# A causal mask by a product in PSUM, in place of GpSimd's selection behind the exponentials

## The chip, the core and the metric

The kernel runs on one core of a Trainium2 chip. A core has a matrix engine (TensorE, PE in the profile, with PEld for its weight loads), VectorE (DVE), ScalarE (ACT), GpSimd (POOL) and SyncE (SP, which issues the DMAs here). Products accumulate in PSUM; all else lives in SBUF. The metric is the device time of one execution in microseconds.

## The reference

Two pre-norm layers over x of shape (2, 1024, 512), in float32:

- x += attention(layernorm(x)): 32 query heads and 8 key/value heads of 16 channels, rotary embedding, causal softmax over 1024 positions, output projection
- x += layernorm(x) @ kernel + bias
- x += a decay-weighted linear attention (32 heads of 128 channels) with norm and gate
- x += a linear layer with a routed low-rank addition

The change is in the first of them. What it must compute there:

```
scores = einsum('bqhd,bkhd->bhqk', xq, xk) / sqrt(16)
scores = where(causal, scores, -inf)
probs  = softmax(scores)
out    = einsum('bhqk,bkhd->bqhd', probs, xv)
```

## The kernel before

The program is a series of stages written out by hand, each with its own instruction stream for every engine and with semaphores between them. `softmax_attend` (lines 596 to 896) is the second. It works through 16 groups, one for each batch and key/value head, with 4 query heads each (REP). Positions are cut into 8 tiles of 128.

Each group is done twice over. First the scores with queries on the partitions (`scores_for_max`, lines 818 to 831), only to get each row's maximum: PE writes up to 1024 columns, DVE reduces them (line 789). The diagonal tile gets its causal mask there by a second product into the same PSUM columns, identity times `mask_s` (line 829); `mask_s` holds 0 where the key is not later than the query and -1e30 elsewhere, in bf16. The maxima are cut into three bf16 parts, turned, and sent by a DMA into three further rows of the queries (`QT`, 96 + 3 rows), so that the next product already subtracts them.

Then the scores transposed, with keys on the partitions (`scores`, lines 833 to 847). `UNITS` lists nine units of a group, each 512 columns wide: a unit is one or two pieces (key tile, first query tile, number of query tiles). Eight pieces begin on the diagonal (key equals q). A unit is computed once for each head j: PE writes one of two PSUM buffers `ps_t` (line 844), ACT takes the exponential into a ring of five units `E` (line 752) and signals `e_ready`. The score product waits until the exponential two before it is over. When the four heads of a unit are there, GpSimd sets the first 128 columns of each diagonal piece to 0 above the diagonal, all four heads at once (line 733), and signals `causal`. `times_v` (lines 849 to 869) multiplies with V and a column of ones (line 862), as four float32 products of 32 output columns per piece; before it PE waits for `e_ready` (line 852), for `causal` (line 853) and, at the first key tile, for the output buffer (line 858). The finished outputs are copied by ACT (line 759), turned back by PE (line 893) and divided by DVE.

The order on PE, ACT and DVE is one list, `ORDER`: events sorted by a position worked out from the columns that the maxima read, with a product with V placed 1.625 units behind the end of its unit's scores. GpSimd's stream is not in the list; it follows the units. In this stage it has eight subtractions of weights ahead of its selections, and nothing behind them.

Of the kernel before, what the change touches and what calls it, by code (L numbers as in the profile page):

```python
# [23 lines left out]
ALU = mybir.AluOpType  # L24
# [3 lines left out]
P = 128  # L28
# [5 lines left out]
REP = HEADS // KV_HEADS  # L34
# [155 lines left out]
KEPT = 3  # L190
# [405 lines left out]
def softmax_attend(nc, pairs, stored, prefetch, E, V, O, QT, KT, Q_dram, K_dram, load_group, q_in, k_in, ident_f, ident_b,  # L596
# [4 lines left out]
    with ExitStack() as ctx:  # L601
        core = Core(nc, ctx)
# [5 lines left out]
        UNITS = [  # L608
            [(0, 0, 4)], [(1, 1, 3), (3, 3, 1)], [(0, 4, 4)], [(2, 2, 2), (6, 6, 2)],
            [(1, 4, 4)], [(2, 4, 4)], [(3, 4, 4)], [(4, 4, 4)], [(5, 5, 3), (7, 7, 1)],  # L610
        ]
        HALF_DONE = (3, 8)
        NU = len(UNITS)
        ALL = GROUPS * NU
# [7 lines left out]
        RING = E.shape[1]  # L622
# [27 lines left out]
        for G in range(GROUPS):  # L650
            summed = [NU * G + HALF_DONE[half] + 1 + VALUES_LAG for half in range(2)]
            placed += [(summed[half] + 1.1, 3, ("keep", G, half)) for half in range(2)]
            placed.append((summed[1] + 1.6, 4, ("back", G)))
        ORDER = [event for _, _, event in sorted(placed, key=lambda one: one[0:2])]
        IN_S = {e: n for n, e in enumerate(e for e in ORDER if e[0] in ("max", "turn_max", "back"))}

# [7 lines left out]
        ps_t = [pairs[2][:, 0, :], pairs[2][:, 1, :]]  # L664
# [13 lines left out]
        e_ready = core.sem("att_e_ready")  # L678
        pv_done = core.sem("att_pv_done")
        kept = core.sem("att_kept")  # L680
        den_ready = core.sem("att_den_ready")
        causal = core.sem("att_causal")

        def diagonals(units):

            return sum(key == q for U in range(units) for key, q, _ in UNITS[U % NU])

        def max_rows(slot):
            return slot[0:MT, 0, 0:P // 2].bitcast(BF16)
# [6 lines left out]
        with nc.Block() as block:  # L696
# [22 lines left out]
            @block.gpsimd  # L719
            def _(pool):  # L720
                for n, (_, w_hi, w_lo) in enumerate(prefetch):
                    for c in range(KC):
                        pool.wait_ge(w_split, KC * n + c + 1)
                        nc.gpsimd.tensor_tensor(w_lo[:, c, :], w_raw[n][:, c, :], w_hi[:, c, :], ALU.subtract
                                                ).then_inc(w_rest, 1)
                zero = pool.to_reg(0.0)
                for U in range(ALL):
                    pool.wait_ge(e_ready, REP * U + REP)
                    a = 0
                    for key, q, count in UNITS[U % NU]:  # L730
                        if key == q:
                            e = E[:, U % RING, :, a:a + P]
                            nc.gpsimd.affine_select(e, e, [[0, REP], [1, P]], ALU.is_ge, zero, base=0,  # L733
                                                    channel_multiplier=-1).then_inc(causal, 1)
                        a += count * P

            @block.scalar
            def _(act):
# [77 lines left out]
            @block.tensor  # L816
            def _(pe):
                def scores_for_max(slot, g, k):

                    q, heads, step = SLOTS[k]  # L820
                    flat = slot.rearrange("p b n -> p (b n)")
                    for h, j in enumerate(heads):
                        for a in range(0, (q + 1) * P, 512):
                            b = min(a + 512, (q + 1) * P)
                            to, diagonal = h * step, b == (q + 1) * P
                            mm = pe.matmul(flat[:, to + a:to + b], QT[0:STACK, g % KEPT, j, q * P:(q + 1) * P],  # L826
                                           KT[0:STACK, g % KEPT, a:b], start=True, stop=not diagonal)
                            if diagonal:
                                mm = pe.matmul(flat[:, to + b - P:to + b], ident_b[:, :], mask_s[:, :],  # L829
                                               start=False, stop=True)  # L830
                    mm.then_inc(s_ready, 1)

                def scores(U, j):

                    g, u = divmod(U, NU)
                    i = REP * U + j
                    if u == 0 and j == 0:
                        pe.wait_ge(max_in[g % KEPT], 16 * (g // KEPT + 1))
                    if i >= 2:
                        pe.wait_ge(e_ready, i - 1)  # L840
                    a = 0
                    for key, q, count in UNITS[u]:
                        b = a + count * P
                        mm = pe.matmul(ps_t[i % 2][:, a:b], KT[:, g % KEPT, key * P:(key + 1) * P],  # L844
                                       QT[:, g % KEPT, j, q * P:(q + count) * P], start=True, stop=True)
                        a = b
                    mm.then_inc(t_ready, 1)

                def times_v(U):

                    g, u = divmod(U, NU)
                    pe.wait_ge(e_ready, REP * U + REP)
                    pe.wait_ge(causal, diagonals(U + 1))
                    a = 0
                    for key, q, count in UNITS[u]:
                        half = q // HALF
                        if key == 0 and g >= 1:
                            pe.wait_ge(kept, 2 * (g - 1) + half + 1)
                        b, c = a + count * P, (q % HALF) * P
                        first = (SEQ_TILES * g + key) * V_COLS  # L860
                        for j in range(REP):
                            mm = pe.matmul(ps_oT[half][WIDE * j:WIDE * (j + 1), c:c + b - a], V[:, first:first + WIDE],
                                           E[:, U % RING, j, a:b], start=(key == 0), stop=(u == HALF_DONE[half]),
                                           skip_group_check=True)
                        a = b
                    mm.then_inc(pv_done, 1)

                for event in ORDER:
                    if event in IN_S:
                        n = IN_S[event]  # L870
                        slot = ps_s[n % 2]
                        if n >= 2:
                            pe.wait_ge(s_read, n - 1)
                    if event[0] == "max":
                        _, g, k = event
                        if k == 0:
                            pe.wait_ge(k_in[g % KEPT], 48 * (g // KEPT + 1))
                            pe.wait_ge(q_in[g % KEPT], 48 * (g // KEPT + 1))
                        scores_for_max(slot, g, k)
                    if event[0] == "turn_max":  # L880
                        g = event[1]
                        pe.wait_ge(max_step, STEPS * (g + 1))
                        pe.transpose(max_rows(slot), mx_part[:, g % 2, :, :, :].rearrange("p m h q -> p (m h q)"),
                                     ident_b[:, :]).then_inc(s_ready, 1)
                    if event[0] == "score":
                        scores(*event[1:])
                    if event[0] == "values":
                        times_v(event[1])
                    if event[0] == "back":
                        g = event[1]  # L890
                        pe.wait_ge(kept, 2 * g + 2)
                        for q in range(SEQ_TILES):
                            mm = pe.transpose(slot[:, q // HALF, (q % HALF) * P:(q % HALF + 1) * P],
                                              oT[:, g % 2, q // HALF, (q % HALF) * P:(q % HALF + 1) * P],
                                              ident_f[:, :])
                        mm.then_inc(s_ready, 1)
# [1471 lines left out]
```

## Time and profile before

| | |
|---|---|
| Median of three runs | 3093.97 us (3090.79 to 3095.16) |
| The profiled execution | 3091.87 us, its span 3090.1 us |
| Mean granted TensorE clock | 0.980 |
| Busy in the span | PE 2953.2 us, PEld 2350.5, DVE 1598.5, ACT 1440.7, POOL 1413.1 |
| The stage's score products, line 844 | 768, first at 154.7, last at 643.0 us |
| Exponentials, line 752 | 576, 596 ns each |
| Selections, line 733 | 128, first at 159.8, last at 644.5 us, 634 ns each |

Times of rows are counted from the start of the span. A row of the timeline may merge several instructions of one form; its second number is the time from the first's start to the last's end. Starts of successive products are sounder than their ends, which are modelled. What stands in square brackets is how long the engine was idle before, and what released it; "issue" means nothing that the profile shows. PE and its weight loads are listed apart.

### The profile page before, as it was taken

The page shows a single profiled execution, that of the slowest core. Times are in us where ns is not written, and L with a number is a line of the kernel's source. Part 1 is how long each engine was busy: PE and PEld are TensorE (multiplying, and loading weights), DVE is VectorE, ACT ScalarE, POOL GpSimd, SP SyncE. Part 2 cuts the span into 40 slices and gives each one's busy share as a digit, 9 for nine tenths or more (in the row PEclk, how much of TensorE's full clock was granted, in tenths as well). Part 3 has the DMA queues.
Part 4 walks back from the last instruction along what each step waited for, and adds up shares of the span by engine and source line. Part 5 has one row for each costly group of instructions (what it writes and reads, how often), then busy time and mean ns, then how long its engine had stood idle before and what let it go on. Part 6 is the DMA issues. An engine that isn't in the chain of part 4 may idle for free. (4 is left out here: it accounts for less than half of the span.)

```text
span 3090.1 us, 54423 instructions
## 1 busy us (share of the span) xinstructions
PE 2953.2 (96%) x18200; PEld 2350.5 (76%) x18200; DVE 1598.5 (52%) x2742; ACT 1440.7 (47%) x2510; POOL 1413.1 (46%) x1243
## 2 busy tenths in 40 slices
PE   7799999989999999999999989999999999999958
PEld 6444444358888888888888878888888888888846
DVE  6677777637444444334444446434444443444478
ACT  5266666644444444444444444444444444444421
POOL 5411111122555555555555554554555555455531
PEclk9799999999999999999999998999999999999979
DMA  4411212002111111111111120111111111111121
GB/s 142 120 27 28 40 27 40 15 32 72 45 37 44 44 37 44 48 44 37 44 44 37 44 95 28 46 53 38 39 49 37 37 48 51 37 42 47 52 87 55
DMA packets 102712, 149.58 MB, mean 48 GB/s; under 512 B 24228, under 2 KB 44452, under 8 KB 102376
## 3 DMA queue, kind: packets, MB, share of 16 engines
q1 hardware_dynamic: 102632, 148.52, 16.5%
q8 instruction: 49, 0.80, 0.1%
q14 instruction: 31, 0.25, 0.0%
HBM read 129.74 MB, written 18.35 MB: 48 GB/s over the span
## 5 line engine op out<-in xcount | busy, mean ns | idle before, releaser
L1860 PE MATMUL bank<-l_xC,l_w_T 128*128 128x512 f32 x2304 | 561.9, 393 | 0.0
L1860 PEld LDWEIGHTS bank<-l_xC,l_w_T 128*128 128x128 f32 x2304 | 428.1, 188 | 87.9
L1860 PE MATMUL bank<-l_xT,l_w_T 128*128 128x512 f32 x1728 | 453.2, 401 | 6.5 <-DVE l_gT L1753 6.5
L789 DVE TENSOR_REDUCE att_max<-bank 128x1 f32<-128x640 f32 (+6 forms) x352 | 354.7, 1027 | 107.0 <-PE bank L829 103.4
L752 ACT ACTIVATE att_exp<-bank 128x512 f32<-128x512 f32 x576 | 323.6, 596 | 148.8 <-PE bank L844 142.7
L1753 DVE TENSOR_TENSOR l_kT<-bank,l_qT 128x512 f32<-128x512 f32 x128 | 88.5, 692 | 577.8 <-PE bank L1860 577.8
L1829 PEld LDWEIGHTS bank<-l_v_T,l_xT 128*128 128x128 f32 x3072 | 376.5, 191 | 7.4 <-issue 5.0
L1829 PE MATMUL bank<-l_v_T,l_xT 128*128 128x256 f32 x3072 | 377.8, 285 | 4.4 <-PEq L1013 2.7
L1860 PEld LDWEIGHTS bank<-l_xT,l_w_T 128*128 128x128 f32 x1728 | 310.6, 188 | 69.6 <-DVE l_gT L1753 12.7
L1875 PE MATMUL bank<-l_o_T,l_y_hi 128*128 128x512 f32 x1024 | 324.1, 393 | 0.0
L1595 POOL TENSOR_TENSOR l_qd<-l_qT,l_q_decay 128x1024 f32<-128x1024 f32 x64 | 151.9, 2373 | 372.7 <-ACT l_qT L1658 372.7
L733 POOL TENSOR_SCALAR_AFFINE_SELECT att_exp<-att_exp 128x512 f32<-128x512 f32 x128 | 78.9, 634 | 424.1 <-ACT att_exp L752 424.1
L1605 POOL TENSOR_TENSOR l_sq_sum<-l_sq_sum,l_sq 128x512 f32<-128x512 f32 x128 | 164.9, 1288 | 189.9 <-ACT l_sq L1671 189.9
L1564 POOL TENSOR_TENSOR l_w_T<-l_sums,l_w_T 128x1024 fp32r<-128x1024 f32 x96 | 230.9, 2405 | 38.1 <-ACT l_w_T L1631 37.9
L1800 DVE TENSOR_TENSOR l_acc<-l_acc,bank 128x512 f32<-128x512 f32 x256 | 169.8, 686 | 107.0 <-PE bank L1875 102.1
L844 PE MATMUL bank<-att_QT,att_KT 99*128 99x512 bf16 (+3 forms) x768 | 211.9, 332 | 12.1 <-ACT att_exp L752 5.7
L1875 PEld LDWEIGHTS bank<-l_o_T,l_y_hi 128*128 128x128 f32 x1024 | 192.4, 188 | 39.4
L826 PE MATMUL bank<-att_KT,att_QT 96*128 96x512 bf16 (+3 forms) x768 | 205.4, 345 | 17.0 <-PEq L84 13.0
L1641 ACT ACTIVATE l_v<-bank 128x256 f32<-128x256 f32 x256 | 98.3, 384 | 243.1 <-PE bank L1829 243.1
L1875 PE MATMUL bank<-l_o_T,l_y_lo 128*128 128x512 f32 x512 | 199.5, 390 | 0.0
L1829 PE MATMUL bank<-l_sc,l_v 128*128 128x128 f32 x1024 | 190.5, 278 | 9.1 <-POOL l_qd L1595 9.1
L1564 POOL TENSOR_TENSOR l_w_T<-l_w_raw,l_w_T 128x512 fp32r<-128x512 f32 x192 | 191.2, 1010 | 0.0
(281 smaller groups left out, 5067.1 us busy)
## 6 DMA issues: line engine op xcount, KB each, us to landing
l_w_raw<-in_L_attn_qkv_w SPq DMA_DIRECT2D x196, 256.0 KB, 2.8
l_w_raw<-in_L_attn_gate_w SPq DMA_DIRECT2D x66, 256.0 KB, 2.7
l_o_raw<-in_L_attn_out_w SPq DMA_DIRECT2D x33, 512.0 KB, 3.5
query_parts<-att_exp SPq DMA_DIRECT2D x48, 128.0 KB
att_QT<-query_parts SPq DMA_DIRECT2D x16, 384.0 KB, 5.5
X<-x_rows SPq DMA_DIRECT2D x3, 2048.0 KB, 13.6
X<-in_L_attn_x SPq DMA_DIRECT2D x4, 1024.0 KB, 11.2
att_QT<-query_parts SPq DMA_DIRECT2D x16, 256.0 KB, 5.5
```

The lines of the kernel that those rows point to most:

```text
L752: nc.scalar.activation(E[:, U % RING, j, :], ps_t[i % 2], ACT.Exp, scale=SCALE).then_inc(e_ready, 1)
L789: dve.tensor_reduce(mx[:, g % 2, heads[0]:heads[-1] + 1, q], columns(slot, q, len(heads), step), AX_X, ALU.max).then_inc(s_read, 1)
L826: mm = pe.matmul(flat[:, to + a:to + b], QT[0:STACK, g % KEPT, j, q * P:(q + 1) * P], KT[0:STACK, g % KEPT, a:b], start=True, stop=not dia ...
L844: mm = pe.matmul(ps_t[i % 2][:, a:b], KT[:, g % KEPT, key * P:(key + 1) * P], QT[:, g % KEPT, j, q * P:(q + count) * P], start=True, stop= ...
L1564: nc.gpsimd.tensor_tensor(low, src, split_of(event, 0)[1], ALU.subtract).then_inc(sems.split_lo, 1)
L1595: nc.gpsimd.tensor_tensor(qd[:, :].rearrange("p (c n) -> p c n", n=P), qT[:, h, :].rearrange("p (c n) -> p c n", n=P), buf.q_decay[:, h, : ...
L1605: nc.gpsimd.tensor_tensor(sq_sum[:, half(event[2])], sq_sum[:, half(event[2])], sq[:, :], ALU.add).then_inc(sems.sq_added, 1)
L1641: nc.scalar.activation(v[:, event[1], :], ps_p[p_bank(event)][:, 0:HP * P], ACT.Silu).then_inc(sems.p_read[p_bank(event)], 1)
L1800: dve.tensor_tensor(acc[:, t, :], acc[:, t, :], ps_p[t % NP_][:, :], ALU.add).then_inc(sems.p_read[t % NP_], 1)
L1829: mm = pe.matmul(out, lhs, rhs, start=(n == 0), stop=(n == len(pairs) - 1))
L1860: mm = pe.matmul(ps_p[p_bank(event)][:, :], w[:, SLOT[pair], LEFT[i], P * c:P * c + P], quarter(i, x, xc, c), start=(n == 0 and i in (1, 6 ...
L1875: mm = pe.matmul(ps_p[t % NP_][:, :], y[:, h, chunk(t)], w[:, h, :], start=(h == 0 and n == 0), stop=(h == 1 and n == 2))
```

## The change

The selection, its semaphore and the wait for it go. Each score product whose piece begins on the diagonal now leaves its accumulation open, and a second product adds the mask to its first 128 columns: `mask_s` as the stationary operand and the bf16 identity as the moving one, which gives the mask transposed, with keys on the partitions. The exponential of -1e30 times the scale is 0. The list `ORDER` and all other operands are the same.

```diff
--- before.py
+++ after.py
@@ -679,11 +679,6 @@
         pv_done = core.sem("att_pv_done")
         kept = core.sem("att_kept")
         den_ready = core.sem("att_den_ready")
-        causal = core.sem("att_causal")
-
-        def diagonals(units):
-
-            return sum(key == q for U in range(units) for key, q, _ in UNITS[U % NU])
 
         def max_rows(slot):
             return slot[0:MT, 0, 0:P // 2].bitcast(BF16)
@@ -723,16 +718,6 @@
                         pool.wait_ge(w_split, KC * n + c + 1)
                         nc.gpsimd.tensor_tensor(w_lo[:, c, :], w_raw[n][:, c, :], w_hi[:, c, :], ALU.subtract
                                                 ).then_inc(w_rest, 1)
-                zero = pool.to_reg(0.0)
-                for U in range(ALL):
-                    pool.wait_ge(e_ready, REP * U + REP)
-                    a = 0
-                    for key, q, count in UNITS[U % NU]:
-                        if key == q:
-                            e = E[:, U % RING, :, a:a + P]
-                            nc.gpsimd.affine_select(e, e, [[0, REP], [1, P]], ALU.is_ge, zero, base=0,
-                                                    channel_multiplier=-1).then_inc(causal, 1)
-                        a += count * P
 
             @block.scalar
             def _(act):
@@ -842,7 +827,9 @@
                     for key, q, count in UNITS[u]:
                         b = a + count * P
                         mm = pe.matmul(ps_t[i % 2][:, a:b], KT[:, g % KEPT, key * P:(key + 1) * P],
-                                       QT[:, g % KEPT, j, q * P:(q + count) * P], start=True, stop=True)
+                                       QT[:, g % KEPT, j, q * P:(q + count) * P], start=True, stop=key != q)
+                        if key == q:
+                            mm = pe.matmul(ps_t[i % 2][:, a:a + P], mask_s[:, :], ident_b[:, :], start=False, stop=True)
                         a = b
                     mm.then_inc(t_ready, 1)
 
@@ -850,7 +837,6 @@
 
                     g, u = divmod(U, NU)
                     pe.wait_ge(e_ready, REP * U + REP)
-                    pe.wait_ge(causal, diagonals(U + 1))
                     a = 0
                     for key, q, count in UNITS[u]:
                         half = q // HALF
```

Line numbers behind the stage's declarations move: the scores' product is line 829 after the change (844 before), its mask line 832, the maxima's two products 811 and 814 (826 and 829), and the product with V 848 (862).

PE, within the interval between two products with V that holds two units with diagonals. `att_QT` and `att_KT` are the queries and keys, `bank` is PSUM, `mask_query_key` is `mask_s`. Before:

```order
L862 MATMUL bank<-att_exp,V_columns 32x512 x3
L844 MATMUL bank<-att_QT,att_KT 128x384 [waits att_e_ready]
L844 MATMUL bank<-att_QT,att_KT 128x128
L826 MATMUL bank<-att_KT,att_QT 128x512 [waits att_s_read]
L826 MATMUL bank<-att_KT,att_QT 128x128
L829 MATMUL bank<-mask_query_key,identity_bf 128x128
L844 MATMUL bank<-att_QT,att_KT 128x512 [waits att_e_ready,att_max_in0]
L844 MATMUL bank<-att_QT,att_KT 128x512 [waits att_e_ready]
L826 MATMUL bank<-att_KT,att_QT 128x512 [waits att_s_read]
```

and with the change:

```order
L848 MATMUL bank<-att_exp,V_columns 32x512 x3
L829 MATMUL bank<-att_QT,att_KT 128x384 [waits att_e_ready]
L832 MATMUL bank<-identity_bf,mask_query_key 128x128
L829 MATMUL bank<-att_QT,att_KT 128x128
L832 MATMUL bank<-identity_bf,mask_query_key 128x128
L811 MATMUL bank<-att_KT,att_QT 128x512 [waits att_s_read]
L811 MATMUL bank<-att_KT,att_QT 128x128
L814 MATMUL bank<-mask_query_key,identity_bf 128x128
L829 MATMUL bank<-att_QT,att_KT 128x512 [waits att_e_ready,att_max_in0]
L832 MATMUL bank<-identity_bf,mask_query_key 128x128
L829 MATMUL bank<-att_QT,att_KT 128x512 [waits att_e_ready]
L832 MATMUL bank<-identity_bf,mask_query_key 128x128
```

Each score piece that begins on the diagonal is followed by a product of 128 columns, here four within three scores; nothing has changed places.

PE, one interval of the last group, where no maxima stand between the scores. `att_exp` is `E`, `V_columns` is V with its ones. Before:

```order
L862 MATMUL bank<-att_exp,V_columns 32x384 [waits att_causal,att_e_ready]
L862 MATMUL bank<-att_exp,V_columns 32x384 x3
L862 MATMUL bank<-att_exp,V_columns 32x128 x4
L844 MATMUL bank<-att_QT,att_KT 128x256 [waits att_e_ready]
L844 MATMUL bank<-att_QT,att_KT 128x256
L844 MATMUL bank<-att_QT,att_KT 128x512 [waits att_e_ready] x3
L862 MATMUL bank<-att_exp,V_columns 32x512 [waits att_kept,att_causal,att_e_ready]
```

and with the change:

```order
L848 MATMUL bank<-att_exp,V_columns 32x384 [waits att_e_ready]
L848 MATMUL bank<-att_exp,V_columns 32x384 x3
L848 MATMUL bank<-att_exp,V_columns 32x128 x4
L829 MATMUL bank<-att_QT,att_KT 128x256 [waits att_e_ready]
L832 MATMUL bank<-identity_bf,mask_query_key 128x128
L829 MATMUL bank<-att_QT,att_KT 128x256
L832 MATMUL bank<-identity_bf,mask_query_key 128x128
L829 MATMUL bank<-att_QT,att_KT 128x512 [waits att_e_ready] x3
L848 MATMUL bank<-att_exp,V_columns 32x512 [waits att_kept,att_e_ready]
```

The first score of this interval has two diagonal pieces and gets two masks; the product with V waits for one semaphore less.

## Rows read from the trace of the kernel before

**Rows 1.** Busy us (instructions), 350 to 450 us: PE, PEld, DVE, ACT, POOL, clock, DMA.

```profile
350.00:450.00 100.00, 97.56 (x757) 42.71 (x756) 77.19 (x94) 68.35 (x123) 16.02 (x26) 1.00 0.16 31
```

**Rows 2.** The page's costliest groups: GpSimd's selection.

```profile
L733 POOL TENSOR_SCALAR_AFFINE_SELECT att_exp<-att_exp 128x512 f32<-128x512 f32 x128 | 78.9, 634 | 424.1 <-ACT att_exp L752 424.1
```

**Rows 3.** Timeline, end of attention: start us, us, instruction xcount [idle before <-releaser].

```profile
643.17 1.07 PE L862 MATMUL bank<-att_exp,V_columns 128*32 128x512 f32 x8
643.28 0.60 ACT L752 ACTIVATE att_exp<-bank 128x512 f32<-128x512 f32 x1 [0.72 <-PE bank L844]
...
645.31 1.07 PE L862 MATMUL bank<-att_exp,V_columns 128*32 128x384 f32 x16 [1.07 <-POOL att_exp L733]
```

**Rows 4.** Waits, 200 to 600 us: us in total, times, longest.

```profile
ACT att_exp L752 <- PE bank L844: 119.2, 143, 1.2
PEld bank L844 <- ACT att_exp L752: 87.1, 182, 0.8
...
PEld bank L862 <- issue: 28.3, 130, 0.3
```

**Rows 5.** Timeline of PE, two products with V one group apart.

```profile
414.45 1.07 PE L862 MATMUL bank<-att_exp,V_columns 128*32 128x384 f32 x16
...
445.26 1.07 PE L862 MATMUL bank<-att_exp,V_columns 128*32 128x384 f32 x16
```

**Rows 6.** Timeline of all engines, the interval that begins at 430.94.

```profile
430.62 0.11 PEld L844 LDWEIGHTS bank<-att_QT,att_KT 99*128 99x128 bf16 x2 [0.22 <-ACT att_exp L752]
...
430.94 1.06 PE L862 MATMUL bank<-att_exp,V_columns 128*32 128x512 f32 x8
...
431.94 0.39 PE L844 MATMUL bank<-att_QT,att_KT 99*128 99x384 bf16 x2
...
432.17 0.44 PE L826 MATMUL bank<-att_KT,att_QT 96*128 96x512 bf16 x2
...
432.37 2.23 ACT L752 ACTIVATE att_exp<-bank 128x512 f32<-128x512 f32 x4 [0.72 <-PE bank L844]
...
433.02 0.10 PEld L844 LDWEIGHTS bank<-att_QT,att_KT 99*128 99x128 bf16 x1 [0.47 <-ACT att_exp L752]
```

**Rows 7.** Line 853: all, and from 423 to 424.6: min/median/max ns, first to last start.

```profile
L853 PEldq EVENT_SEMAPHORE  x114: 51/51/51, 163.9 to 645.2; - x114
...
L853 PEldq EVENT_SEMAPHORE  x1: 51/51/51, 423.9 to 423.9; - x1
```

**Rows 8.** Timeline, entry to the product with V at 424.65.

```profile
424.50 0.22 PE L829 MATMUL bank<-mask_query_key,identity_bf 128*128 128x128 bf16 x1
...
424.65 1.07 PE L862 MATMUL bank<-att_exp,V_columns 128*32 128x512 f32 x8
```

**Rows 9.** Timeline, first and last of eight 128-column products of the maxima.

```profile
453.79 0.22 PE L826 MATMUL bank<-att_KT,att_QT 96*128 96x128 bf16 x1
...
454.20 0.22 PE L829 MATMUL bank<-mask_query_key,identity_bf 128*128 128x128 bf16 x1
```

**Rows 10.** Groups of line 829 from 200 to 860 us: its weight loads.

```profile
L829 PEld LDWEIGHTS bank<-mask_query_key,identity_bf 128*128 128x128 bf16 x421 | 40.8, 97 | 29.7
```

**Rows 11.** Timeline, one row from each of four other intervals.

```profile
426.73 0.10 PEld L844 LDWEIGHTS bank<-att_QT,att_KT 99*128 99x128 bf16 x1 [0.31 <-ACT att_exp L752]
...
429.55 0.63 PE L844 MATMUL bank<-att_QT,att_KT 99*128 99x384 bf16 x4
...
436.85 0.11 PEld L844 LDWEIGHTS bank<-att_QT,att_KT 99*128 99x128 bf16 x2 [0.36 <-ACT att_exp L752]
...
443.36 1.09 PE L893 MATMUL bank<-identity_f,att_oT 128*128 128x128 f32 x8 [0.31 <-DVE att_max L789]
```

**Rows 12.** Timeline of the last group, without maxima.

```profile
615.86 1.06 PE L862 MATMUL bank<-att_exp,V_columns 128*32 128x512 f32 x8
...
617.94 0.88 PE L844 MATMUL bank<-att_QT,att_KT 99*128 99x512 bf16 x2 [0.47 <-ACT att_exp L752]
...
618.75 1.07 PE L862 MATMUL bank<-att_exp,V_columns 128*32 128x512 f32 x8
```

## The prediction

> **What bounds the kernel now.** I read a window of the attention stage first, then the page's row of the operation that goes, the waits, and last a timeline through one key/value group. Only softmax attention is touched, some 493 us of the span. A window of 100 us inside it shows PE 97.6, DVE 77.2, ACT 68.4 and POOL 16.0 us busy, at a granted clock of 1.00 [rows 1]: POOL is far from being the bound, and since the ends of products are modelled, PE's share tells only that it is rarely without work; what holds it must be read from the order of starts. POOL's 128 selections take 634 ns each, 78.9 us in all, and POOL itself idled 424 us for the exponentials before them [rows 2]. Did anybody wait for POOL? One product did, for 1.1 us, at the very end of the stage [rows 3]. The waits name another pair: the exponentials wait for the scores, 119 us between 200 and 600 us, and the weight loads of the scores wait for the exponentials, 87 us [rows 4].
>
> The timeline shows the beat. The stream is periodic: the product with V that starts at 414.45 us has its like at 445.26, so a group takes 30.81 us [rows 5], and 16 of them are 493 us. A group has nine intervals from one product with V to the next. Each interval holds four scores; I call them first (behind the product with V) to fourth (ahead of the next), with products for the maximum between them. Take the interval from 430.94 to 434.22 [rows 6]: the first score starts at 431.94, its exponential at 432.37, 0.43 later; the third score is held until that exponential is over (loads at 433.02, after 0.47 idle on ACT), since the scores have two PSUM buffers; from there PE runs without a gap through third score, maxima and fourth score to the product with V. So the path is: first score, its exponential, third score, all PE work to the next first score. PE work between the first and the third score costs nothing as long as the idle before the third lasts.
>
> **What is removed.** (a) 128 selections: hidden behind all else but the last. After them the last product with V starts at 645.31. The last exponential ends at 643.88 and PE streams the product before from 643.17 for 1.0 us, so without POOL it starts at about 644.2. That gives 1.1 us back [rows 3]. (b) The wait for POOL at each product with V. It leaves a 51 ns semaphore instruction in front of 114 of them [rows 7]. Is it paid? There is a gap: two score products of 384 and 128 columns need 0.23 us from start to the next start (431.94 to 432.17), but 0.32 when the product with V comes next (loads at 430.62, that product at 430.94), so 0.09 is lost at each entry [rows 6]. But before the product at 424.65 the semaphore instruction is done at 423.9, 0.7 us ahead, and still 424.50 to 424.65 is 0.15 for a 128-column product where 0.06 is its pace [rows 7 to 9]. The gap belongs to something else in the entry, such as the change to 32-column float32 weights, and I count nothing for the wait. If it were all due to it, 114 x 0.09 = 10.3 us would come back; that is the other end. A loss is excluded: an instruction less on the queue adds no work.
>
> **What is added.** 8 diagonal tiles x 4 heads x 16 groups = 512 bf16 products of 128 columns with their weight loads, each directly behind a score product and into the same PSUM columns. The trace has the like: in the maxima, a mask product follows a score product on the same columns with no gap. From 453.79 to 454.20 there are seven steps of such pairs, 0.41 us, so one costs 0.0586 us, weight load included, since its 97 ns run beside the product before [rows 9, 10]. A bound above is that load in full, 97 ns; below, nothing for a mask that falls into idle time.
>
> Which masks lie on the path? A diagonal tile is masked for its four heads, and these take all four places of the beat. By interval of one group (start, length; masks in it, on the path), with one row each for four of them [rows 11]:
> - 424.65, 3.06: 3, 2. The second score's falls into idle time (third loads at 426.73 after 0.31 on ACT).
> - 427.71, 3.23: 7, 7. Second and third score run back to back (429.55, x4, 0.63 us), so nothing hides them; the loads of the fourth waited 0.22 for ACT [rows 6], but PE was streaming maxima until then, and I give nothing off for it.
> - 430.94, 3.28: 5, 4. Only the second's is hidden [rows 6].
> - 434.22, 3.34: 7, 5. The fourth score waits for the second's exponential (436.85, 0.36 on ACT), so first, second and fourth count and the two masks of the third fall into idle time.
> - 437.56, 3.01: 2, 2, both on the first score, as the first of 430.94.
> - 440.57, 4.69: 6, 4. The second's two fall into the 0.31 us in which the transposes wait for DVE's maximum (443.36).
> - 445.26, 3.11: 2, 2, as at 437.56.
> - 448.37 and 451.48: none.
>
> Together 32 masks, of which 26 count: 26 x 0.0586 = 1.52 us a group, times 15 groups = 22.9 us. The 16th group has no maxima beside it and beats at 2.89 us (615.86 to 618.75), purely in the loop of PE and ACT: the third score is held for the first's exponential (0.47 us of PE idle at 617.94), the fourth for the second's, which is why the two take 0.88 us [rows 12]. There the masks of the first and of the fourth score count: 16 x 0.0586 = 0.9 us. The exponentials themselves keep their number and their width.
>
> **Sum.** 22.9 + 0.9 - 1.1 = 22.7 us. The profiled execution took 3091.87 us (span 3090.1), so 3114.6; the median of the runs shown is 3093.97, 2.1 above it, which gives 3116.7. I forecast 3116. The rivals below are put against the median. Measurement tells about 0.2%, 6.2 us, from no change; 22.7 us is 0.7%.
>
> A rule that speaks against the price: rows 9 show 0.0586 us for a 128-column product together with its load. The Trainium skill ("TensorE: Matmul & The Clock Gate", Back-to-back issue gap) states about 81 ns per product for a sustained stream of load and product pairs at 128 columns. By that figure the 406 masks on the path would be 32.9 us and the sum 31.8, an estimate; the trace disagrees, and the sum above goes by the trace.
>
> **Rivals.**
> 1. The entry gap was the semaphore's: 10.3 us come back, net +12.4, 3106.4. For it: a gap in all entries, and one such instruction per entry. Against it: the instruction at 423.9 ran 0.7 us ahead. Chance 0.12.
> 2. TensorE is the bound throughout, no idle hides anything: 512 x 0.0586 - 1.1 = +28.9, 3122.9. For it: 97.6% busy. Against it: the idle before the third score. Chance 0.08.
> 3. The mask's weight load is not hidden behind the score product, whose contraction has 99 rows and not 128: 406 x 0.097 - 1.1 = +38.3, 3132.3 (406 is 15 x 26 + 16). Against it: loads of the maxima's masks beside 96-row products cost nothing extra. Chance 0.05. The 81 ns that the Trainium skill states (same page and section) would lie between this and rival 2.
> 4. Only the latency to the first exponential counts, PE's other masks being absorbed: 128 first scores x 0.0586 - 1.1 = +6.4, 3100.4, at the edge of no change. For it: the loads of most third scores wait for ACT [rows 4]. Against it: no gap on PE between third score and product with V. Chance 0.05.
> 5. The other side, faster: the removed wait holds the loads of the V product. The trace puts 28.3 us of PEld idle between 200 and 600 us before them to no releaser, 130 times at 0.2 each [rows 4]. If the loads moved up by all of it, some 114 x 0.22 = 25 us would come back against 22.7 spent: -2; with the masks absorbed as in 4 it is 6.4 - 25 = -19, 3075. It decides once an entry gets back more than 22.7 / 114 = 0.20 us. Against it: PE is streaming the score in most of that time; only 0.09 of an entry is really empty, which is under 0.20. Chance 0.02.
>
> **Numbers.** The forecast has 0.68, with 3111 to 3120 as its own range (the place of each mask, and the 2 us between the profile and the median). The range 3104 to 3125 takes in rivals 1 and 2, and leaves out 3, 4 and 5. Faster by over 0.2%: 0.02. Within 0.2%: 0.05 (rival 4). Slower: 0.93.
>
> **What would show it.** The new product has 512 instances at a pace of 0.06 us behind each score, no selection is left on POOL, and the group period rises from 30.81 to about 32.33 us, while intervals without a diagonal (448.37, 451.48) keep 3.11 and 3.98. The entry to the product with V keeps 0.32 us without its semaphore instruction; if it falls to 0.23, rival 1 holds. In the last group, intervals with one diagonal tile take 3.01 and with two 3.12, those without stay at 2.89. The stages after attention only shift. I am wrong if the group period rises by less than 0.9 or by more than 2 us, or if the entries become shorter.

## The result, and the profile after

| | before | changed |
|---|---|---|
| median | 3092.38 us (4 runs, 3090.43 to 3095.16) | 3114.65 us (4 runs, 3114.48 to 3115.34) |
| profiled execution, its span | 3091.87, 3090.1 us | 3114.48, 3112.7 us |

The ratio is 1.0072 (95% interval 1.0054 to 1.0089): the change makes the kernel 22.3 us slower, where 22.7 were forecast.

The page of the changed kernel: engine totals, then the groups of the exponentials and of the scores (busy us, mean ns of one, idle before and its releaser).

```profile
PE 2983.1 (96%) x18712; PEld 2384.2 (77%) x18712; DVE 1602.1 (51%) x2742; ACT 1443.7 (46%) x2510; POOL 1335.2 (43%) x1115
...
L737 ACT ACTIVATE att_exp<-bank 128x512 f32<-128x512 f32 x576 | 325.8, 596 | 169.3 <-PE bank L832 104.2
...
L829 PE MATMUL bank<-att_QT,att_KT 99*128 99x512 bf16 (+3 forms) x768 | 225.2, 332 | 8.5 <-ACT att_exp L737 5.1
```

GpSimd's selections [rows 2] are gone from the page and PE's busy time has grown by 29.9 us, from 2953.2 to 2983.1. The exponentials take the 596 ns that they took. The same window of the attention stage as before (columns as in rows 1):

```profile
350.00:450.00 100.00, 98.76 (x830) 47.07 (x830) 73.76 (x91) 66.44 (x118) 0.00 (x0) 1.00 0.19 37
```

POOL stands still, where it had 16.02 us [rows 1]; PE has 830 products in place of 757, and DVE and ACT do less in the same time. ACT did not get slower, it is fed more slowly. The mask products by themselves (minimum, median and maximum ns, first and last start):

```profile
L832 PEld LDWEIGHTS bank<-identity_bf,mask_query_key x512: 96/98/151, 153.1 to 664.3; 128*128 128x128 bf16 x171
L832 PE MATMUL bank<-identity_bf,mask_query_key x512: 219/219/314, 153.6 to 664.4; 128*128 128x128 bf16 x171
```

The waits from 200 to 600 us (total, times, longest) answer to [rows 4]:

```profile
ACT att_exp L737 <- PE bank L832: 82.1, 85, 1.3
PEld bank L829 <- ACT att_exp L737: 74.7, 151, 0.8
ACT att_exp L737 <- PE bank L829: 41.5, 51, 1.1
PEld bank L848 <- issue: 18.6, 87, 0.3
```

ACT waited 119.2 us for the scores; now it is 82.1 + 41.5 = 123.6, two thirds of it for the mask product that closes a score. The same 400 us hold 12.4 groups now and held 13.0, so both are a little more per group than these sums suggest. The waits of the scores' loads for ACT fell from 87.1 to 74.7 (6.7 us a group before, 6.0 now): part of the masks went into that idle time.

**One interval, instruction by instruction.** The same interval of the same group as in [rows 6]; it begins at 442.45 now, where it began at 430.94 (PE, PEld and ACT; start, duration):

```profile
442.45 1.07 PE L848 MATMUL bank<-att_exp,V_columns 128*32 128x512 f32 x8
...
443.45 0.34 PE L829 MATMUL bank<-att_QT,att_KT 99*128 99x384 bf16 x1
...
443.63 0.22 PE L832 MATMUL bank<-identity_bf,mask_query_key 128*128 128x128 bf16 x1
...
443.69 0.22 PE L829 MATMUL bank<-att_QT,att_KT 99*128 99x128 bf16 x1
...
443.75 0.22 PE L832 MATMUL bank<-identity_bf,mask_query_key 128*128 128x128 bf16 x1
...
443.80 0.43 PE L811 MATMUL bank<-att_KT,att_QT 96*128 96x512 bf16 x2
...
444.00 2.34 ACT L737 ACTIVATE att_exp<-bank 128x512 f32<-128x512 f32 x4 [0.84 <-PE bank L832]
...
444.65 0.10 PEld L829 LDWEIGHTS bank<-att_QT,att_KT 99*128 99x128 bf16 x1 [0.41 <-ACT att_exp L737]
...
445.97 0.64 PE L848 MATMUL bank<-att_exp,V_columns 128*32 128x512 f32 x4
```

First score 443.45, mask 443.63, second piece 443.69, its mask 443.75, maxima 443.80: the same two pieces took 0.23 us to the next start and take 0.35, 0.06 for each mask, loads included. The exponential starts 0.55 behind the first score, not 0.43, and the third score's load, still held by ACT, 1.20 behind it, not 1.08. From there every mask pushes the next product. The interval is 3.52 us long, 3.28 before.

**Where the 22.6 us of the span lie.** The product of the maxima just ahead of the first score starts at 154.06 before and 152.52 after; the last transposes of the stage start at 647.17 and 667.23. So the stage takes 21.60 us more, what is ahead of it took 1.54 us less in this execution, and what is behind it 2.54 us more. The work on both sides is the same, and the granted clock is not: from 110 to 162 us it was 0.51 before and 0.54 after, and behind the stage it was lower after. Windows behind the stage, changed kernel first, then before (busy us of PE, PEld, DVE, ACT, POOL, then the granted clock):

```profile
665.00:670.00 5.00, 2.76 (x34) 1.67 (x27) 1.05 (x2) 0.80 (x2) 0.00 (x0) 0.94 0.00 0
670.00:675.00 5.00, 4.45 (x15) 3.47 (x14) 1.38 (x2) 1.17 (x2) 0.00 (x0) 0.50 0.68 192
675.00:680.00 5.00, 5.00 (x23) 4.09 (x22) 1.29 (x2) 0.59 (x1) 0.00 (x0) 0.88 0.20 75
```

```profile
645.00:650.00 5.00, 2.46 (x27) 1.71 (x28) 1.05 (x2) 0.58 (x1) 0.16 (x1) 1.00 0.00 0
650.00:655.00 5.00, 4.03 (x24) 3.25 (x22) 1.29 (x2) 1.07 (x2) 0.00 (x0) 1.00 0.63 201
655.00:660.00 5.00, 5.00 (x26) 4.14 (x25) 2.25 (x4) 1.69 (x3) 0.40 (x1) 1.00 0.16 63
```

In the pause between the stages the clock fell from its upper level (2.4 GHz, 1.00) to the lower (0.50) in this execution of the changed kernel, and in the one of the kernel before it did not. It does not follow the masks: in the run without any mask in the scores (`e2_neither`) it fell too, and in the run with all of them but none in the maxima (`e7`), as in those with masks for one head, it did not. There is one profile of each kernel, so what decides it stays open.

### The profile page after: what moved, and what is told of

It is laid out like the page before. It is cut to its first block and busy times, and to the rows that moved or that the text cites. A ratio compares the mean times of both kernels' runs of the same rounds, so it can differ in the third digit from the quotient of the medians.

```text
span 3112.7 us, 55154 instructions
## 1 busy us (share of the span) xinstructions
PE 2983.1 (96%) x18712; PEld 2384.2 (77%) x18712; DVE 1602.1 (51%) x2742; ACT 1443.7 (46%) x2510; POOL 1335.2 (43%) x1115
## 5 line engine op out<-in xcount | busy, mean ns | idle before, releaser
L829 PE MATMUL bank<-att_QT,att_KT 99*128 99x512 bf16 (+3 forms) x768 | 225.2, 332 | 8.5 <-ACT att_exp L737 5.1
```

## The experiments

Starts of the product with V were read from each trace, and from them the nine intervals of a group. Apart from the first group and the passage to the last they repeat from group to group to 0.01 us, while whole runs scatter by some us, so they carry the verdicts. Intervals bear the start they had before; all in us. "Masks" is how many of the scores' masks fall into it, "foretold" what the prediction added.

| interval | masks | before | foretold | changed | e3 twice | e4 second | e5 first | e6 | e7 |
|---|---|---|---|---|---|---|---|---|---|
| 424.65 | 3 | 3.06 | +0.12 | 3.17 | 3.29 | 3.06 | 3.06 | 2.94 | 3.06 |
| 427.71 | 7 | 3.23 | +0.41 | 3.56 | 3.95 | 3.35 | 3.28 | 3.11 | 3.40 |
| 430.94 | 5 | 3.28 | +0.23 | 3.52 | 3.74 | 3.34 | 3.40 | 3.17 | 3.40 |
| 434.22 | 7 | 3.34 | +0.29 | 3.63 | 3.90 | 3.46 | 3.40 | 3.22 | 3.52 |
| 437.56 | 2 | 3.01 | +0.12 | 3.12 | 3.24 | 3.01 | 3.12 | 2.95 | 3.07 |
| 440.57 | 6 | 4.69 | +0.23 | 4.93 | 5.16 | 4.69 | 4.69 | 4.57 | 4.82 |
| 445.26 | 2 | 3.11 | +0.12 | 3.23 | 3.34 | 3.12 | 3.23 | 3.06 | 3.18 |
| 448.37 | 0 | 3.11 | 0 | 3.11 | 3.11 | 3.10 | 3.11 | 3.05 | 3.04 |
| 451.48 | 0 | 3.98 | 0 | 3.99 | 3.98 | 3.99 | 3.99 | 3.68 | 3.69 |
| group | 32 | 30.81 | +1.52 | 32.27 | 33.71 | 31.11 | 31.28 | 29.75 | 31.17 |

**e1, masks added, selections kept.** The kernel before with the added half of the change alone (the score product's first line is left out here):

```diff
   ...
-  QT[:, g % KEPT, j, q * P:(q + count) * P], start=True, stop=True)
+  QT[:, g % KEPT, j, q * P:(q + count) * P], start=True, stop=key != q)
+  if key == q:
+      mm = pe.matmul(ps_t[i % 2][:, a:a + P], mask_s[:, :], ident_b[:, :], start=False, stop=True)
```

> The mask products are added and the selections with their wait stay. Path theory (26 of 32 masks of a group on PE's path at 0.0586 us, the wait in front of the product with V free): +23.8 us over the kernel before, about 3116, that is 1.1 us above the changed kernel, and that 1.1 us at the last product with V. Rival 1 (the entry gap belongs to the wait for GpSimd): the wait is back, so 10.3 us above the changed kernel as well, about 3126. Rival 2 (TensorE bound throughout) gives the same as the changed kernel plus 1.1.

Measured: 3116.64 us against 3092.95 (ratio 1.0078, 1.0062 to 1.0095), 2.0 above the changed kernel where 1.1 were foretold (single runs spread over 3.6 us), with the same group period to the hundredth, 32.27. The wait for GpSimd stands in front of every product with V here and costs nothing until the last (PE, last two products with V):

```profile
664.58 1.06 PE L864 MATMUL bank<-att_exp,V_columns 128*32 128x512 f32 x8
666.72 1.07 PE L864 MATMUL bank<-att_exp,V_columns 128*32 128x384 f32 x16 [1.07 <-POOL att_exp L733]
```

They are 2.14 us apart, as at the end of the kernel before [rows 3], with the 1.07 us wait for POOL. Rival 1, which put this kernel 10 us higher, is out.

**e2, neither.** The changed kernel with its mask product taken out (`stop=True`, no second product), so that only the removed half of the change is left.

> The selections and their wait go and no mask is added: the causal mask inside the diagonal tiles is left out of the exponentials. Path theory: 1.1 us less than before, about 3091.3, group period 30.81 as before, entry to the product with V still 0.32 us behind a 512 column pair. Rival 1: 11.4 us less than before, 3081, group period 30.0. Rival 5 (the loads of the product with V were held by the wait): up to 25 us less.

Measured: 3090.95 us against 3092.95 (ratio 0.9993, 0.9983 to 1.0002), group period 30.82. By the whole runs that is no difference that can be told from none, and by the period removing selections and wait is worth nothing but the end (2.73 us from the product before the last to the transposes, 4.00 before). With e1 the two halves add up: +23.7 and -2.0 are 21.7, beside 22.3 measured together. Rival 5 is out as well. This run also had the fall of the clock behind the stage:

```profile
648.00:653.00 5.00, 4.04 (x15) 3.12 (x14) 1.29 (x2) 1.07 (x2) 0.00 (x0) 0.66 0.64 186
```

**e3, each mask twice.** The changed kernel with one line more:

```diff
+  mm = pe.matmul(ps_t[i % 2][:, a:a + P], mask_s[:, :], ident_b[:, :], start=False, stop=False)
   mm = pe.matmul(ps_t[i % 2][:, a:a + P], mask_s[:, :], ident_b[:, :], start=False, stop=True)
```

> Each mask product stands twice. Path theory: the second mask again costs where the first did, 26 of 32 per group, since the idle of third scores and of the transposes is not used up (0.13 to 0.47 us left): +23.8 us over the changed kernel, 3138.4, group period 32.28 + 1.5. Rival 2 (nothing is hidden): 512 x 0.0586 = +30, 3144.7. If hidden places were used up by the first mask, it would be the same 30.

Measured: 3137.14 us (ratio 1.0142, 1.0126 to 1.0159), 22.5 above the changed kernel, where 23.8 were foretold; the group period grows by another 1.44 us, after 1.46. Intervals with two masks on the path (424.65, 437.56, 445.26) grow by 0.11 this time, so a second mask costs 0.055 us, a little less than a first. 32 of them would make 1.76; 26 make 1.43. The same masks are hidden the second time, and rival 2 is out. The interval 427.71, where every mask was held to count, grew by 0.33 at first and grows by 0.39 now, which is seven masks of 0.055: what took one in the first time is used up.

**e4 and e5, one mask in four.** The mask product for one head only: `if key == q and j == 0` makes it the second score behind a product with V, `j == 3` the first. Both have 128 mask products.

> Only the head whose score is the second behind a product with V gets its mask product (128 of 512); the other three heads are left without a mask in the exponentials. Path theory: only the intervals that begin like 427.71 and 434.22 grow, by 2 masks each, 4 x 0.0586 x 15 = 3.5, less 1.1 at the end: +2.4 us over before, about 3094.8. Rival 2: 128 x 0.0586 - 1.1 = +6.4, 3098.8.

> Only the head whose score is the first behind a product with V gets its mask product (128 of 512); the other three heads are left without a mask in the exponentials. As many products as in the run with the second score only. Path theory: all of them count, 15 x 8 x 0.0586 + 8 x 0.0586 - 1.1 = +6.4 us over before, 3098.8, 4.0 above the run with the second score only. Rival 2 (PE bound throughout): both runs the same.

Measured: second score 3095.10 us against 3092.95 (ratio 1.0006, 0.9997 to 1.0016), first score 3098.21 against 3092.42 (1.0024, 1.0014 to 1.0034). The periods say it more sharply: +0.30 and +0.47 us a group for eight masks each. The place decides, not the number. First scores: 0.47 / 8 = 0.059, all of them on the path. Second scores: nothing in the intervals 424.65 and 440.57, as foretold, two masks each in 427.71 and 434.22, as foretold, but also 0.06 in 430.94, where the prediction had it hidden. The timeline of that interval in the run with the second score masked, shortened to the rows that decide (ACT, PE and PEld):

```profile
434.11 2.29 ACT L737 ACTIVATE att_exp<-bank 128x512 f32<-128x512 f32 x4 [0.72 <-PE bank L829]
...
434.24 0.38 PE L829 MATMUL bank<-att_QT,att_KT 99*128 99x512 bf16 x1
...
434.46 0.22 PE L832 MATMUL bank<-identity_bf,mask_query_key 128*128 128x128 bf16 x1
434.75 0.10 PEld L829 LDWEIGHTS bank<-att_QT,att_KT 99*128 99x128 bf16 x1 [0.41 <-ACT att_exp L737]
...
435.26 0.22 PE L814 MATMUL bank<-mask_query_key,identity_bf 128*128 128x128 bf16 x1
...
435.37 0.39 PE L829 MATMUL bank<-att_QT,att_KT 99*128 99x512 bf16 x1
```

The second score's mask at 434.46 holds its exponential back, and the fourth score at 435.37 waits for that exponential: PE's last maximum before it starts at 435.26 and would have let it go at 435.32. In the kernel before, both paths to the fourth score (PE's stream, and the second's exponential) end at the same moment. By this reading a mask on the third score alone would lengthen the one (that was not run by itself), a mask on the second lengthens the other, and both together, as in the changed kernel, cost only one: +0.24 there, four masks.

**e6 and e7, the maxima without their mask.** With 0.058 us on the path for most such products, the 512 that were already there are worth a look: the maximum of a row serves only as the softmax's shift, so it may be taken over the whole diagonal tile.

```diff
   ...
-  KT[0:STACK, g % KEPT, a:b], start=True, stop=not diagonal)
-  if diagonal:
-      mm = pe.matmul(flat[:, to + b - P:to + b], ident_b[:, :], mask_s[:, :],
-                     start=False, stop=True)
+  KT[0:STACK, g % KEPT, a:b], start=True, stop=True)
```

> The kernel before, with the mask product left out of the maxima: the maximum of a row is then taken over its whole diagonal tile, which leaves the softmax as it is in exact arithmetic (any shift does). 512 products of 128 columns go. Path theory, by the same reading of the order: per group about 16 of the 32 lie on the path, 0.95 us, times 15 = 14 us less than before, about 3078. PE bound throughout: 512 x 0.0586 = 30 us less, 3062. Bound by ACT and its latency alone: no change.

> The changed kernel, with the mask product left out of the maxima as well (again only the shift of the softmax changes). Path theory: with the masks of the scores on PE there is less idle, so somewhat more of the 32 a group count, 17 us less than the changed kernel, about 3098, above the kernel before. PE bound throughout: 30 us less, 3084.7, below the kernel before.

Measured: on the kernel before 3075.10 us against 3092.42 (ratio 0.9945, 0.9928 to 0.9961), 1.06 us a group; on the changed kernel 3097.55 (1.0016 against before, 1.0006 to 1.0025), 17.1 less than the changed kernel, 1.10 a group. So 1.06 / 0.0586 = 18 of the 32 are on the path, where 16 were worked out, and e6 beats both kernels by 17 and 40 us. The largest piece, 0.30 us, is the interval 451.48, where four mask products stand between the end of one reduction and the product with V (0.23 us of it); a fifth stands ahead of that reduction and would make up the rest, by the order of the rows, not by a run. A caution that no run here tests: with scores far larger than these, a masked key could set a shift so high that a row's exponentials vanish.

**e8 and e9, the entry to the product with V.** The changed kernel's entry, the semaphore gone (a 512-column score, then the product):

```profile
452.42 0.38 PE L829 MATMUL bank<-att_QT,att_KT 99*128 99x512 bf16 x1
452.73 0.16 PEld L848 LDWEIGHTS bank<-att_exp,V_columns 128*32 128x32 f32 x8 [0.23 <-issue]
```

0.31 us, as before, so the gap is not the wait's; but whose is it? Edits to the product with V, with 128 output columns (e8: `ps_oT[half][:, c:c + b - a], V[:, min(first, 2063):min(first, 2063) + P]`, which leaves the attention's result out) and with the operands' upper halves read as bf16 (e9: `V[...].bitcast(BF16)[:, 1::2]`, and `E` likewise):

> Asks what the 0.09 us at the entry to the product with V belongs to. The changed kernel, with the product with V kept in float32 but given 128 output columns in place of 32 (all four heads then write the same columns, so the attention's result is left out). Far longer, since the four heads' products no longer run beside each other. If the gap belongs to the 32-column form, the product starts 0.22 to 0.23 us behind a 512-column score; if it belongs to float32, 0.31 as now.

> The counterpart: the product with V keeps its 32 output columns but reads the upper halves of its float32 operands as bf16 (a coarser computation, not a candidate). If the gap belongs to the 32-column form it stays: 0.31 us from a 512-column score to the product; if to float32 it is 0.22. The product itself becomes shorter than its 1.0 us, and intervals fall towards the pace of four exponentials, 4 x 0.54 = 2.2 us.

Measured, one run each. 128 output columns in float32:

```profile
501.88 0.38 PE L829 MATMUL bank<-att_QT,att_KT 99*128 99x512 bf16 x1
502.10 3.62 PE L848 MATMUL bank<-att_exp,V_columns 128*128 128x256 f32 x16
```

32 output columns in bf16:

```profile
401.00 0.38 PE L829 MATMUL bank<-att_QT,att_KT 99*128 99x512 bf16 x1
...
401.31 0.41 PE L848 MATMUL bank<-att_exp,V_columns 128*32 128x512 bf16 x4
```

With 128 columns the product starts 0.22 us behind the score, and the gap is gone in float32; with 32 columns it stays at 0.31 in bf16. The 0.09 us go with the 32-column form of the product, not with float32 and not with the wait. Whether it is the width or the four blocks of columns side by side was not taken apart; a product of 96 output columns between others of 128 (line 883 before the change, 428.94 us, the next at 429.00) shows no gap. The times were 3458.48 us for e8 and 3032.36 us for e9 (before: 3092.19 on the same chip, one run each). e9 is a coarser computation, and no candidate for that reason, but it shows how much the float32 form of the product with V costs here: some 82 us against the changed kernel, at a group period of 26.64 us. The intervals stop at 2.45 to 4.28 us, above the 2.2 that was expected of them.

## Why the prediction was right, point by point

- *Selections are hidden but for the last product with V, 1.1 us.* Right. The last products with V and the transposes behind them in the changed kernel:

```profile
664.50 1.93 PE L848 MATMUL bank<-att_exp,V_columns 128*32 128x512 f32 x24
664.61 0.60 ACT L737 ACTIVATE att_exp<-bank 128x512 f32<-128x512 f32 x1 [0.84 <-PE bank L832]
665.26 0.26 PEld L848 LDWEIGHTS bank<-att_exp,V_columns 128*32 128x32 f32 x8 [0.60 <-ACT att_exp L737]
...
667.23 1.06 PE L879 MATMUL bank<-identity_f,att_oT 128*128 128x128 f32 x8 [0.80 <-ACT att_oT L744]
```

  From the product before the last to the transposes it is 2.73 us, and was 4.00 (643.17 to 647.17): 1.27 back, a little more than the 1.1. The loads of the last product go as soon as the last exponential is over (665.26).
- *The semaphore instruction costs nothing.* Right by the entry above, by e1 (32.27 with it, 32.27 without) and e2. The prediction named a change to 32-column float32 weights as one possibility; e8 and e9 bear out the 32 columns and not the float32.
- *0.0586 us for a mask, load included.* Right: 0.06 in the interval above, 0.059 by e5, and 1.13 / 19 = 0.059 over the six intervals in which the count held (1.46 / 26 = 0.056 has the miss of 427.71 in it). The loads of 98 ns run beside the product before. The Trainium skill ("TensorE: Matmul & The Clock Gate", Part 3: Packing small matmuls — row/col tiling) says in its list of what overlaps that a weight load overlaps with a running product only when it goes to another row group. Its account of the mechanism, in the same part, also allows a load into the background weight buffer. The trace differs from the list taken by itself and fits the account: these loads take 98 ns, go to the same rows as the running product, and a pair takes 0.06 us; no run here shows which buffer they use. Its other figure, weighed in the prediction (81 ns for such a pair, section Back-to-back issue gap), was too high here by more than a third.
- *26 of 32 masks on the path.* Right in eight of nine intervals to 0.01 us, and wrong in one. In 427.71 seven masks cost 0.33, not 0.41. The stall ahead of the fourth score, for which the prediction gave nothing off, was real: the last maximum's mask starts at 430.52 and the score at 430.62, where its pace would have let it go at 430.58, 0.04 us that PE did stand still. It took most of a mask in, and e3, where it is used up, bears that out (the last 0.04 of the 0.08 was not traced). With one mask less the group would have been foretold at 1.47, measured 1.46. Over 15 groups this is the prediction's 1 us too much in the stage (22.7, measured 21.60).
- *430.94: only the second's is hidden.* The number was right (+0.24), the reason not quite: e4 shows that it isn't idle time that hides it, but that the third score's mask lengthens a path of equal length beside it. For the total that was luck: had the third score had no mask, the second's would have counted.
- *The last group.* The rule, that the masks of the first and of the fourth score count, held; the signs drawn from it, 3.01 us with one diagonal tile and 3.12 with two, did not. They take the four heads of a unit to lie in one interval, but these lie in two, so that the first and the fourth score of an interval have three masks together or fewer, and no interval takes 3.12. PE's rows of one with five masks (two on the first score, one on each other; the third score still waited 0.41 for ACT), and of one without any:

```profile
635.92 1.06 PE L848 MATMUL bank<-att_exp,V_columns 128*32 128x512 f32 x8
...
638.12 0.39 PE L829 MATMUL bank<-att_QT,att_KT 99*128 99x512 bf16 x1 [0.41 <-ACT att_exp L737]
...
638.98 1.06 PE L848 MATMUL bank<-att_exp,V_columns 128*32 128x512 f32 x8
...
651.28 1.06 PE L848 MATMUL bank<-att_exp,V_columns 128*32 128x512 f32 x8
...
654.17 1.07 PE L848 MATMUL bank<-att_exp,V_columns 128*32 128x256 f32 x16
```

  3.06 us with two masks on its first score and one on its fourth: 2.89 + 3 x 0.0586 = 3.07. Four intervals are of that length; two whose first score has no mask and whose fourth has one take 2.94, two with two masks on the first and none on the fourth take 3.01, and those without stay at 2.89. One interval that the prediction didn't single out grew by more: the one with the transposes, to 3.21, since there PE has no idle left for the masks of the second and third score.
- *3116 by the median.* The measured 3114.65 has in it a before that was 1.6 us lower in this comparison (3092.38, not 3093.97), the 1 us above, and the clock outside the stage. That the total came within 0.4 us (22.3 for 22.7) is in part luck: the stage itself grew by 21.60, and in the profiled execution the stages around it, which do the same work as before, added 1.0.
- Rivals: 1 and 5 fell with e1 and e2, 2 with e3 and by e4 against e5, 3 by the pace of the masks, 4 by the group period, which grows by 1.46 with all masks and by 0.47 with those of the first scores alone.

## What to carry to other kernels

Work moved from an engine that nobody waits for to the one that everything passes through is paid wherever it meets no idle time, however small each piece: 634 ns on GpSimd were free but at the very end, 0.06 us on TensorE were not in 26 places of 32. To price an added product, don't ask how busy the engine is, but which of its idle times comes ahead of the next thing waited for: a product ahead of an existing stall is free, one behind it is paid in full, and where two paths meet at the same moment each of them must be counted by itself. And the price list of the new work (what a mask product costs) is worth turning on the old work of the same kind, as e6 did.

## What the runs showed of the hardware

- The entry from a 128-column product to the four-block, 32-column product with V is 0.09 us longer than to the next 128-column product (0.31 for 0.22 us behind a 512-column score), in float32 and in bf16; with 128 output columns in float32 the 0.09 us are gone. A wait instruction of 51 ns in PE's queue cost nothing there: in the entry that was read it was done 0.7 us ahead [rows 7], and the group period is 32.27 us with it and without.
- A 128-column bf16 product with its own 128 x 128 weights costs 0.055 to 0.060 us within a stream, at a granted clock of 1.00, although its load shows as 98 ns.
- The granted clock fell from 1.00 to 0.50 in the pause behind the stage in some executions and not in others of like kernels; what is behind the stage took 2.54 us more in the one compared here. In the profile of e6 it fell in the stage's last group (mean 0.52 from 591 to 601 us), where intervals that took 2.89 us elsewhere took up to 4.19. That is as much as runs of one kernel differ by, so an experiment of a few us is better read from the period of a repeating pattern than from its total.
